# Second attention of a fused two-layer kernel: output projection in one matmul, softmax sums moved by one transfer, the probability-times-value work spread differently over the steps

## The reference, cut to what matters

```
q, k, v = (x @ w.T + b).reshape(B, T, 16, 8)          # for wq, wk, wv
scores  = einsum('bthd,bshd->bhts', q, k) * 8 ** -0.5  # masked keys: -inf
attn    = softmax(scores, axis=-1)
out     = einsum('bhts,bshd->bthd', attn, v).reshape(B, T, 128)
return out @ wo_w.T + wo_b
```

## Time and profile before

| | |
|---|---|
| Median of 3 runs | 1719.5 us (1717.72 to 1721.88) |
| Profiled execution: time, span | 1716.81 us, 1714.8 us |
| Busy, share of the span | PE 91%, DVE 78%, ACT 74%, POOL 56% |
| Granted TensorE clock, mean | 0.961 of full speed |
| Chain that ended last | PE 74%, DVE 9%, issue 9%, ACT 5%, DMA 1% |

### The profile page before, as it was taken

One profiled execution on the slowest core, in us unless ns is written; L12 is line 12 of the kernel. 1 busy time (PEld: TensorE's weight loads), 2 busy tenths in 40 slices (PEclk: granted clock), 3 DMA queues, 4 the chain that ended last, 5 costly groups with the idle time before them and its releaser, 6 DMA issues.

```text
span 1714.8 us, 28178 instructions
## 1 busy us (share of the span) xinstructions
PE 1565.8 (91%) x10531; PEld 653.2 (38%) x10531; DVE 1345.5 (78%) x2075; ACT 1274.7 (74%) x2053; POOL 961.9 (56%) x660
## 2 busy tenths in 40 slices
PE   5899999999999999999999999986675899999985
PEld 2444444444444444444444444434551222222223
DVE  6687777778777777788777877778778999999946
ACT  4777888888888888888888888884252688888872
POOL 2799877878778877878778877880000000111111
PEclk9999999999999999999999999997686899999997
DMA  4010011101011001101010111100000000000001
GB/s 124 23 27 23 21 29 33 25 23 27 22 34 27 23 26 36 26 21 26 24 38 22 23 27 33 23 9 5 1 22 22 8 15 15 15 15 15 15 14 32
DMA packets 50434, 42.35 MB, mean 25 GB/s; under 512 B 26021, under 2 KB 39242, under 8 KB 50298
## 3 DMA queue, kind: packets, MB, share of 16 engines
q1 hardware_dynamic: 50298, 40.55, 9.5%
HBM read 20.27 MB, written 1.31 MB: 13 GB/s over the span
## 4 chain that ended last, share of the span: by engine, by line
PE 74%; DVE 9%; issue 9%; ACT 5%; DMA 1%; POOL 1%; SPq 1%; ACTq 0%; POOLq 0%; DVEq 0%
PE PS L1453 20%; PE PS L1465 16%; PE PS L1477 13%; PE PS L1807 4%; PE PS L1520 4%; PE PS L1501 3%; DVE mxp L1359 2%; PE PS L1774 2%; PE PS L1791 2%; PE PS L1537 2%; PE PS L1491 2%; PE PS L1747 1%; DVE region L1045 1%; ACT region L765 1%; ACT ering L939 1%
## 5 line engine op out<-in xcount | busy, mean ns | idle before, releaser
L1031 DVE TENSOR_REDUCE nmx<-PS 128x1 f32<-128x1024 f32 x512 | 621.6, 1219 | 193.7 <-PE PS L1454 193.2
L569 POOL TENSOR_TENSOR ering<-ering 128x1024 f32<-128x1024 f32 x256 | 603.4, 2357 | 21.4
L747 ACT ACTIVATE ering<-PS,nmx 128x1024 f32<-128x1024 f32 x512 | 570.4, 1114 | 42.2 <-DVE nmx L1031 41.8
L567 POOL TENSOR_SCALAR ering<-ering,rho 128x1024 f32<-128x1024 f32 x256 | 286.6, 1119 | 220.8 <-DVE rho L1040 217.8
L1453 PE MATMUL PS<-region 64*128 64x512 f16 x1536 | 404.1, 380 | 6.2 <-DMA region<-region 4.4
L1454 PE MATMUL PS<-region 64*128 64x512 f16 x1536 | 404.2, 380 | 0.0
L1465 PE MATMUL PS<-ident,ering 128*128 128x128 f32 x2048 | 334.1, 286 | 8.8 <-ACT t L758 6.4
L1359 DVE TENSOR_REDUCE mxp<-PS 128x2 f32<-128x1024 f32 x256 | 303.7, 1220 | 30.6 <-PE PS L1791 26.9
L939 ACT ACTIVATE ering<-PS 128x1024 f32<-128x1024 f32 x256 | 260.4, 1025 | 76.8 <-PE PS L1774 69.2
L1465 PEld LDWEIGHTS PS<-ident,ering 128*128 128x128 f32 x2048 | 215.0, 141 | 258.9 <-issue 220.8
L1453 PEld LDWEIGHTS PS<-region 64*128 64x128 f16 x1536 | 112.4, 94 | 248.8 <-ACT ering L747 72.1
(11 more groups left out here) (286 smaller groups left out, 1855.7 us busy)
## 6 DMA issues: line engine op xcount, KB each, us to landing
region<-region SPq DMA_DIRECT2D x64, 256.0 KB, 3.7
osb<-scr SPq DMA_DIRECT2D x32, 128.0 KB, 3.1
rcp<-scr SPq DMA_DIRECT2D x32, 128.0 KB, 3.2
rcp<-scr SPq DMA_DIRECT2D x64, 64.0 KB, 2.0
x<-in_L_attn_X SPq DMA_DIRECT2D x4, 256.0 KB, 3.2
wq_raw<-in_L_attn_Wq SPq DMA_DIRECT2D x16, 64.0 KB, 3.1
wk_s<-in_L_attn_Wk SPq DMA_DIRECT2D x16, 64.0 KB, 1.9
wo_s<-in_L_attn_Wo SPq DMA_DIRECT2D x32, 32.0 KB, 2.6
```

Of the source, the lines that this page charges most:

```text
L567: P.tensor_scalar(e2, e2, rho[:, s:s + 1], 1.0, ALU.mult, ALU.mult).then_inc(s_scl_ok, 1)
L569: P.tensor_tensor(e1, e1, e2, ALU.subtract).then_inc(s_sub_ok, 1)
L747: A.activation((E1, E2)[p][s % 4], PS[:, bank:bank + 2, :].rearrange("p a b -> p (a b)"), ACT.Exp, bias=nmx[:, 2 * s + p:2 * s + p + 1], s ...
L1031: V.tensor_reduce(nmx[:, 2 * s + p:2 * s + p + 1], PS[:, bank:bank + 2, :].rearrange("p a b -> p (a b)"), AX.X, ALU.max, negate=True).then ...
```

## The change

The output projection of a half becomes one matmul of 512 columns at t = 14 or 30. The four transfers of the sums become one, whose source is four partitions of `osb` and whose destination is all 128 partitions of `rc`. The reciprocal moves in VectorE's queue from behind reduction 7 (23) to behind reduction 5 (21). V does 256 columns in the first step of a half too; the half has 16 such pieces in 15 steps, and the step that does two of them is t = 9 or 25. Only the first piece of a half carries the start flag. The counts on `s_pv1` and `s_sum_dma1` follow.

```diff
             def sums_out1(hf):
                 sp.wait_ge(s_os1_ok, hf + 1)
-                for j in range(4):
-                    sp.dma_start(rc[32 * j:32 * j + 32, 0, :],
-                                 osb[32 * j + 8:32 * j + 9, :].rearrange("o (p c) -> o p c", c=16)).then_inc(s_sum_dma1, 16)
+                sp.dma_start(rc[:, 0, :], osb[8:128:32, :].rearrange("j (p c) -> j p c", c=16)).then_inc(s_sum_dma1, 16)
...
-                    pool.wait_ge(s_pv1, 30 * (n - 1))
+                    pool.wait_ge(s_pv1, 32 * (n - 1))
...
-                act.wait_ge(s_pv1, 15 * (hf + 1))
+                act.wait_ge(s_pv1, 16 * (hf + 1))
...
-                            act.wait_ge(s_pv1, 15 * ((c - 8) // 16) + 2 * ((c - 8) % 16 // 2) + 1)
+                            act.wait_ge(s_pv1, 16 * ((c - 8) // 16) + 2 * ((c - 8) % 16 // 2) + 2)
...
-                dve.wait_ge(s_sum_dma1, 64 * (hf + 1))
+                dve.wait_ge(s_sum_dma1, 16 * (hf + 1))
...
-                    if t == 7 and n >= 1:
+                    if t == 5 and n >= 1:
                         invert1(2 * n - 1)
...
-                    if t == 23 and 0 <= n < last1:
+                    if t == 21 and 0 <= n < last1:
                         invert1(2 * n)
...
             def values1(n, qh, k, half):
-                if k == 0:
+                if k == 0 and half == 0:
...
-                at = slice(256 * half, 256 * half + (HF if k == 0 else 256))
+                at = slice(256 * half, 256 * half + 256)
                 for i in range(4):
                     c = 16 * qh + 2 * k + i % 2
                     mm = MM(OT[32 * i:32 * i + 32, at], vst[:, n % 2, k, i, :], ering[:, c % 8, i // 2, at],
-                            start=(k == 0), stop=(k == 7 and half == 1))
+                            start=(k == 0 and half == 0), stop=(k == 7 and half == 1))
...
-            def to_out1(hf, part):
+            def to_out1(hf):
                 pe.wait_ge(s_on1_ok, hf + 1)
-                at = slice(256 * part, 256 * part + 256)
-                mm = MM(MISC[:, at], wo1[:, hf // 4, :], on[:, at], start=True, stop=True)
-                if part == 1:
-                    mm.then_inc(s_y1_mm, 1)
+                MM(MISC, wo1[:, hf // 4, :], on[:, :], start=True, stop=True).then_inc(s_y1_mm, 1)
...
-                    if t % 16 == 4 and own:
-                        values1(n, t // 16, 0, 0)
-                    if (5 <= t < 19 or t > 20) and own:
-                        values1(n, t // 20, (t - 16 * (t // 20) - 3) // 2, (t - 3) % 2)
+                    if (4 <= t < 19 or t >= 20) and own:
+                        qh = t // 20
+                        v = t - 16 * qh
+                        for q in (v - 4,) if v < 9 else (5, 6) if v == 9 else (v - 3,):
+                            values1(n, qh, q // 2, q % 2)
...
-                    if t in (14, 15) and n >= 1:
+                    if t == 14 and n >= 1:
                         if own:
                             pe.wait_ge(s_ct_ev1, 2 * n + 2)
-                        to_out1(2 * n - 1, t - 14)
+                        to_out1(2 * n - 1)
...
-                    if t in (30, 31) and own:
+                    if t == 30 and own:
                         if nxt:
                             pe.wait_ge(s_ct_ev1, 2 * (n + 1) + 1)
-                        to_out1(2 * n, t - 30)
+                        to_out1(2 * n)
```

## The result

The changed kernel has a median of 1709.8 us against 1719.9 before, five runs each; the ratio is 0.9942 with a 95% interval of 0.9927 to 0.9958, so 7 to 13 us faster. (One of its runs, at 2888 us, is left out of the ratio.) Predicted were 1711.0 us, 8.5 less.

The account below looks back on a forecast made before the run. It took a loop through PSUM banks shared by maxima and scores (2.40 us per two steps), plus stalls on the sums, as the bound. Terms 2.6 + 0.4 + 0.3 + 0.6 + 2.2 + 1.1 + 1.3 = 8.5 us gave 1711.0 us, range 1706 to 1717.5.

Parts of the forecast that it names:

- one matmul, 13 halves: Output projection, n=0 to 6: a 512-column block takes 1.06 us against 1.26, 0.20 saved 13 times, 2.6 us.
- doubled step moved, in A: Values steps between first and last spread1 (A): 0.28 us gained, 0.26 given back per half, some 0.3 us in 14.
- n=7: projection twice, values: In n=7: two shorter projections save 0.4 us; V one step further behind lets exps follow at 0.92, 0.6 us.
- n=7: sums earlier: Step 10 of n=7: one transfer brings the reciprocal and the norm4(0) behind it 2.2 us earlier, all of it counting.
- n=7: clock: Behind step 10 of n=7: shorter TensorE stall keeps the clock up, V back from 1.01 to 0.57; 1.1 us.
- end: sums earlier: After the last half: the reciprocal, with norm4(2) behind it, comes 1.3 us earlier.
- The landing: Single transfer of the sums: dealt by four rows over four engines, lands 2.3 us after issue; ends 1.75 and 3.2.
- The stall and the clock: TensorE at step 10 of n=7: idle time shrinks from 2.88 us to 0.7 or 1.3, and the clock stays up.
- The loop: Second attention's steady part: M(t+2) waits for exp(t) through shared PSUM bank pairs; two steps take 2.40 us.
- The slow rival: Sums landing beyond 2.8 us delay reduction 6 behind the reciprocal in 14 halves; at 4.0, 1731 us; chance 0.08.

Follow-up runs that it names:

- e2: Kernel before with only the output projection as one matmul of 512 columns; ratio to before 0.9981 (0.9969 to 0.9994).
- e1: Kernel before with only the sums moved by one transfer, reciprocal still behind reductions 7 and 23; ratio to before 0.9976 (0.9964 to 0.9988).
- e3: Kernel before with only the values work changed (256-column pieces, doubled step moved, counts on s_pv1); ratio to before 0.9998 (0.9983 to 1.0013).
- e4: Changed kernel with the four transfers of before, reciprocal still behind reductions 5 and 21; ratio to before 1.0057 (1.0036 to 1.0077).
- e10: Changed kernel run once more, unaltered; median 1708.9 us, ratio to before 0.9942 (0.9927 to 0.9956).
- e12: Changed kernel with the reciprocal one reduction earlier, behind 4 and 20; one run, first to last spread1 314.69 us against 311.90.
- e5: Changed kernel with the reciprocal back behind reductions 7 and 23; ratio to before 0.994 (0.9921 to 0.9958).
- e7: Changed kernel with the doubled values step at v = 17 in place of v = 9; ratio to before 0.9918 (0.9899 to 0.9937).
- e11: Changed kernel with the doubled values step at v = 17, run again; median 1704.9 us, ratio to before 0.9918 (0.9903 to 0.9934).

## Why the prediction was right, step by step

| step | predicted | measured |
|---|---|---|
| one matmul, 13 halves | 2.6 | 2.66 (e2 against e1) |
| doubled step moved, in A | 0.3 | 0.31 (e3), 0.41 (beside the projection) |
| n=7: projection twice, values | 0.4 + 0.6 | 0.98 (24.46 to 23.48 from `to_out1(13)` to the last copy of OT) |
| n=7: sums earlier | 2.2 | 2.58; in both, 0.8 is one late landing of before |
| n=7: clock | 1.1 | 1.13 (5.61 to 4.48) |
| end: sums earlier | 1.3 | 1.73 (4.22 to 2.49 from the copy to the reciprocal) |
| not in the sum | | A of before 0.7 longer by chance, behind the last reciprocal 0.4 |
| sum | 8.5 | 10.6 |

**The landing** was mis-sized: 2.3 us taken, 1.87 measured, 1.8 being the old ones'. The mechanism, dealing out by four rows over four engines, is what the packets show. But the price of a piece was read from the 0.19 us in which any engine was busy. The digits of that row add up to some 0.09 us of work per engine, or 10 ns for each of nine packets (estimate); the rest is that the engines didn't work at the same moment. So the mechanism cost 0.1 us and not 0.6, and both ends gained 0.4 more each.

**Luck.** In n=7 the old fourth transfer landed late in the profiled execution, 2.59 us, while in e2, e3 and e4 the reciprocal came 0.8 sooner. That part is no gain of the change, and the forecast had it too: its 2.2 us were read off this very landing, and would have been 1.4 with one on time. The window of 1640.3 to 1643 us of the kernel before has that landing and the late one before it (2.4 is their median), and one packet of the instruction queue, 16 KB:

```profile
q8 instruction: 1, 0.02, 2.0%
...
rc<-osb SPq DMA_DIRECT2D x2, 2.0 KB, 2.4
```

The four traces with the old transfers (before, e2, e3, e4) have 256 of them, of which 51 landed later than 1.9 us. In each of these 51 a packet of the instruction queue, of 8 or 16 KB, started between 1 us ahead of the issue and the landing; of the 205 on time 19 had one. That it causes the delay is argued from this and was not tried. Without the 0.8 and the 0.7 of A, the change is worth 9.1 us in these two profiles, and the forecast without the 0.8 was 7.7. The medians of the runs are 10.1 us apart, 9.2 with e10.

**The stall and the clock.** The tile was 2.6 us earlier and TensorE found 0.87 us of idle time. Behind 2.88, 2.64, 2.63 and 2.06 us the granted clock was 0.69 in the mean of the next 5.5 us, partly the level of 1.2 GHz, with 5.6 us to the projection; behind 1.34, 0.87 and 0.29 it was 1.00, with 4.15 to 4.58 us. The expectation rested on a single row with 0.55 us; the runs bear it out on both sides.

**The loop.** The 2.40 us of two steps and what TensorE, ScalarE and VectorE add to it held in every run. That V(20) is bound by the copy, exp(20) by the copy of the maxima and M(18) by the copy of y gave the projection's 0.20 in full. The doubled step costs 0.24 in the loop (0.26 worked out), and its net of 0.02 per half came out as 0.02 in e3 and 0.03 beside the projection.

**The slow rival** needed sums later than 2.8 us behind the copy. They came at 1.9. e4 made them come at 3.6, and the kernel was slower than before, by the mechanism, the place and the rate of the rival. In e12 the wait stood one reduction earlier, and 0.57 us of it were free. So the early reciprocal is safe only with the single transfer, and in the halves it brings no time by itself, only the wider margin of POOL's product.

**Open.** From the last reciprocal to the end it is 31.7 us after, 32.0 before, 30.1 in e1, 29.3 in e5 and 33.4 in e3, by code that hardly differs; e7 and e11 are one kernel and have 31.6 and 33.4. So none of it is put down to the change. One part is seen: VectorE's four operations of `norm4` (L1313) take 2.06 us in most runs and 1.11 in e1 and e5. The first three take 0.34 us each everywhere; the fourth takes 1.3 where it starts at or up to 0.1 us behind the start of POOL's product, and ends with it, and 0.34 where it starts 0.1 to 0.2 ahead of it. That the product holds it up is argued from these rows and was not tried by itself. The rest goes with the granted clock, which is low for a varying part of this stretch. Why the stage starts up to 7 us apart was not looked into; it lies ahead of the change.

## What to carry to other kernels

Where three engines are within some per cent of each other, find the loop through their shared buffers, add up its durations, and walk every edit through it: block sizes from the timeline gave the steady part to 0.2 us in 300. A transfer's worth is read where something long is queued behind its consumer; here it was worth nothing in 14 halves and some 5 us in two places, 0.8 of them by chance. An operation that waits for a transfer may be moved forward in a queue only up to the landing: 0.3 us beyond it was free in e4, then it was paid for in full in every half. And a landing is a spread, not a number: the four transfers were on time in one trace's half and 1.3 us late in the next.

## What was not expected of the hardware

- 32 pieces of 64 B on each of four DMA engines landed in 1.87 us, two on each of 16 in 1.75 to 1.8.
- The last of four per-tile operations on VectorE took 1.3 us in place of 0.34 when it started at or up to 0.1 us behind the start of POOL's elementwise product of 512 columns (11 traces), and 0.34 when it started 0.1 to 0.2 us ahead of it (e1, e5).
- 51 of 256 small transfers landed 0.2 to 1.4 us late, all of them beside a packet of the instruction queue of 8 or 16 KB; of the 205 on time 19 had such a packet.
